# Four attention and expert layers in one kernel: a shorter start, and attention without loops in the first and the last layer

## The chip, the cores and the metric

The kernel runs on one core of a Trainium2 chip. The metric is the time of one execution on the device, in microseconds; three runs of the kernel before gave 761.37, 761.84 and 765.79, with a median of 761.84. Lower is better.

## The reference

Four layers follow each other on a residual stream x of 1024 tokens (4 sequences of 256) by 128 features. Each layer adds a cross-attention to a context of 4 x 64 tokens and then a mixture of experts:

```
x = x + xattn_0(layernorm(x), ctx, ctx, fside)     # 16 heads of 8, bias fside (256 x 64)
x = x + ffn_0(layernorm(x))                        # 8 experts, top 2, capacity 320
x = x + xattn_1(ctx, ctx, layernorm(x))            # exponential features
x = x + ffn_1(layernorm(x))                        # 16 experts that choose 64 tokens, shared expert
x = x + xattn_2(...);  x = x + ffn_2(layernorm(x)) # 16 heads of 8; 16 experts, top 2, dense
x = x + xattn_3(layernorm(x), ctx, ctx)            # 16 heads of 64
x = x + ffn_3(layernorm(x))                        # 8 experts, top 1
```

The attention of layers 0 and 3 is, per head h:

```
q = xn Wq_h,  k = ctx Wk_h,  v = ctx Wv_h
P = softmax(q k^T * scale + bias);  out = concat_h(P v) Wo
```

## The kernel before

Tokens lie in T = 8 tiles of 128 rows. Every engine has its own program, and the order of the work is written out by hand; the engines meet only in semaphores. Two tiles are in flight, with buffers j = 0 and 1 (scores in PSUM banks 2j and 2j + 1, turned probabilities in banks 4 and 5, outputs in bank 6 + j).

**Start.** GpSimd (POOL) makes some forty constants, among them `ident`, the head masks `hm8`, `hm16`, `hm64`, and clears `Vb`; its last instruction (L414) raises `const`, and all engines wait for that. SyncE queues the loads: x, the context three times, `aw0` (the attention weights of layer 0), `fside`, the rest, then padding stores and the expert weights of layer 0. VectorE (DVE) runs `setup()` (L1565 to L1598), and then `stats(0)`, the layer norm's mean and variance; GpSimd raises the variance to -0.5 (L457).

**Keys.** The query weights are folded into the keys: `A[:, b, h, :] = Wq_h^T k_h`, so that scores are one matmul of the turned, normalised x with A. For it TensorE (PE) projects the context (L594) into bank 0, ScalarE (ACT) copies it to `projT`, GpSimd multiplies each of 4 sequences' keys by the head mask into 16 blocks of 64 columns (`kblk`, L429), TensorE multiplies those by Wq (L603, eight matmuls of 128 rows and 512 columns), and ScalarE copies them into A. `v_sb` counts the copies of the values into `Vb`, where each head has 9 columns, the last a one that yields the softmax's sum.

**Attention of layers 0 and 3.** For a tile: `norm_x` (DVE, L1619), transpose (PE, L650), `x_out` (ACT), scores (PE, L653), `softmax_in` (DVE, L1629 to L1639: scale and bias in layer 0, maxima, subtract), `exp` (ACT, L1318), in layer 3 `den` (DVE, L1650 and L1652) and `normalise` (POOL, L545), `turn` (PE, eight transposes, L667), `turned` (ACT), `values` (PE, L682 with 18 columns or L679 with 128), in layer 0 `norm_out` (DVE), `turn_out` (PE, L689), `out_turned` (ACT), `project` (PE, L695), and `residual` (DVE, L1672). Each engine has a function `tile_step`, of which four run inside a hardware loop of two turns. TensorE's step for tile g is: transpose and scores of tile g + 2, turn g, turn out g - 1, values g, project g - 1. VectorE's is: norm_x g + 2, norm_out g - 1 (or den g), softmax_in g + 1, residual g - 1. The layers 1 and 2 have attention functions of their own.

After the attention comes `stats(1)`, `route(0)` (xn, router matmuls L887, maxima from L1817), and the experts.

## Time and profile before

| | |
|---|---|
| median of 3 runs | 761.84 us (761.37 to 765.79) |
| the profiled execution | 759.42 us, span 757.3 us |
| busy in the span | PE 491.4 (65%), DVE 303.0 (40%), ACT 176.8 (23%), POOL 182.1 (24%) |
| mean granted TensorE clock | 0.81 of 2.4 GHz |
| the chain that ended last | PE 44%, DVE 19%, issue 12%, POOL 9%, DMA 8%, ACT 7% |
| DMA | 42.15 MB, mean 56 GB/s |

Busy shares are means over stages with different limits. The chain of waits goes back from the last instruction to what released it, and its shares say who held the end up.
### The profile page before, as it was taken

The numbers are of one execution on the slowest core, as the hardware profiler recorded it, in microseconds if no ns is written. First come the engines' busy times: TensorE is split into PE (matmuls) and PEld (weight loads), VectorE is DVE, ScalarE is ACT, GpSimd is POOL, SyncE is SP. The second block draws the span as 40 slices with busy tenths as digits, with TensorE's granted clock in tenths as the row PEclk, the third lists the DMA queues.
The fourth block names the chain that finished last, engine by engine and source line by source line (L and its number), as shares of the span: only waits on it lengthen the run. The fifth ranks groups of instructions, "written<-read, shape, count | busy, mean of one in ns | idle before, by whom it ended". The sixth has DMA issues, their size and how long they took to land.

```text
span 757.3 us, 7336 instructions
## 1 busy us (share of the span) xinstructions
PE 491.4 (65%) x2438; PEld 301.5 (40%) x2440; DVE 303.0 (40%) x754; ACT 176.8 (23%) x366; POOL 182.1 (24%) x194
## 2 busy tenths in 40 slices
PE   1788842267925886664678816758997978650883
PEld 1265631244712444442345513433333535440562
DVE  1755546501243454477122212645442067531221
ACT  1432300022410311200132312302113533300431
POOL 6400000074570000000355531000002623314232
PEclk9997755577976897585899975959999999955897
DMA  7700000032440000101266520000103020003200
GB/s 233 270 1 0 1 29 2 1 83 89 164 128 1 0 1 1 32 0 29 60 198 198 151 60 1 1 0 1 33 30 148 1 90 0 0 1 110 65 13 4
DMA packets 29459, 42.15 MB, mean 56 GB/s; under 512 B 7060, under 2 KB 23581, under 8 KB 29298
## 3 DMA queue, kind: packets, MB, share of 16 engines
...
## 4 chain that ended last, share of the span: by engine, by line
PE 44%; DVE 19%; issue 12%; POOL 9%; DMA 8%; ACT 7%; another core or an unknown queue 0%; POOLq 0%; DVEq 0%; ACTq 0%; SPq 0%
DMA residual<-eo,idx 4%; PE bank L653 3%; PE bank L982 3%; PE bank L747 3%; DMA xgr<-rows,idx 2%; PE bank L990 2%; PE bank L1027 2%; DVE ind L1941 2%; PE bank L1031 2%; POOL pr L545 2%; PE bank L682 2%; PE bank L887 2%; PE bank L1023 2%; DVE PT L1723 2%; PE bank L903 2%
## 5 line engine op out<-in xcount | busy, mean ns | idle before, releaser
L457 POOL TENSOR_TENSOR rstd<-ve,neghalf 128x8 f32<-128x8 f32 x8 | 13.2, 1652 | 211.2 <-DVE ve L1562 211.1
L1239 ACT ACTIVATE PT<-bank 128x512 f32<-128x512 f32 x48 | 27.2, 596 | 74.9 <-PE bank L667 54.3
L653 PE MATMUL bank<-A,xaT 128*128 128x512 f32 (+1 forms) x64 | 37.6, 718 | 7.5 <-ACT xaT L1239 7.5
L448 POOL TENSOR_TENSOR kblk<-projT,hm 128x512 f32<-128x512 f32 x16 | 16.7, 1041 | 85.5 <-ACT projT L1239 85.4
L520 POOL DMA_INDIRECT residual<-eo,idx x16 | 25.3, 1579 | 36.6 <-DMA residual<-eo,idx 21.0
L2027 DVE SCALAR_TENSOR_TENSOR PT<-bank,xgr,sg 128x512 f32<-128x512 f32 x16 | 12.0, 751 | 51.8 <-ACT sg L1470 51.8
L491 POOL DMA_INDIRECT A<-rows,from_row x20 | 19.2, 960 | 53.1 <-DVE from_row L1875 47.3
L903 PE MATMUL bank<-ind,ones_bf 128*128 128x56 bf16 (+1 forms) x160 | 12.9, 240 | 29.3 <-DVE ind L1941 29.3
L982 PE MATMUL bank<-pr,wbig 128*128 128x320 f32 x64 | 26.1, 497 | 7.4 <-issue 6.7
...
L2056 DVE TENSOR_TENSOR PT<-bank,sg 128x352 f32<-128x352 f32 x15 | 7.9, 525 | 49.8 <-ACT sg L1504 49.8
L667 PE MATMUL bank<-ident,pr 128*128 128x128 f32 x128 | 19.8, 305 | 11.1 <-POOL pr L545 8.8
L667 PEld LDWEIGHTS bank<-ident,pr 128*128 128x128 f32 x128 | 16.8, 159 | 21.6 <-issue 9.7
L497 POOL DMA_INDIRECT choices<-eo,to_row x20 | 19.7, 987 | 21.4 <-DVE eo L1992 17.4
L545 POOL TENSOR_TENSOR pr<-pr,rden 128x1024 f32<-128x1024 f32 x8 | 15.2, 1902 | 39.9 <-DVE rden L1652 39.9
L903 PEld LDWEIGHTS bank<-ind,ones_bf 128*128 128x128 bf16 x160 | 9.6, 120 | 37.0 <-DVE ind L1941 36.4
L571 POOL DMA_INDIRECT result<-lg,Vb x15 | 14.8, 984 | 39.8 <-DVE lg L2061 39.8
L990 PE MATMUL bank<-PT,wbig 128*128 128x320 f32 x64 | 24.1, 467 | 0.0
L2001 DVE COPY yT<-bank 128x320 f32<-128x320 f32 x8 | 3.9, 491 | 48.0 <-PE bank L990 48.0
L1984 DVE TENSOR_TENSOR PT<-bank,sg 128x512 f32<-128x512 f32 x16 | 11.1, 692 | 29.0 <-ACT sg L1421 29.0
L1239 ACT ACTIVATE A<-bank 128x512 f32<-128x512 f32 (+1 forms) x24 | 12.6, 526 | 39.2 <-PE bank L823 22.7
L747 PE MATMUL bank<-A,kblk 128*128 128x512 f32 x32 | 19.4, 753 | 3.1 <-ACT kblk L1362 3.1
...
## 6 DMA issues: line engine op xcount, KB each, us to landing
...
wbig<-in_fw SPq DMA_DIRECT2D x8, 512.0 KB
wbig<-in_aw SPq DMA_DIRECT2D x1, 2048.0 KB, 10.0
...
```

The lines of the kernel that those rows point to most:

```text
L448: pool.tensor_tensor(out=kblk[:, c % 2, 0:512].rearrange("p (b h k) -> p b h k", b=B, h=2), in0=projT[:, c % 2, :].rearrange("p (b k) -> p ...
L491: pool.indirect_dma_start(xgr0[:, 5 * p + k, :], None, rowd0, bass.IndirectOffsetOnAxis(from_row[:, 5 * p + k:5 * p + k + 1], 0)).then_inc ...
L497: pool.indirect_dma_start(yd, bass.IndirectOffsetOnAxis(to_row[:, 5 * p + k:5 * p + k + 1], 0), eo0[:, 5 * (p % 2) + k, :], None, bounds_c ...
L520: pool.indirect_dma_start(xd, bass.IndirectOffsetOnAxis(idx[:, e:e + 1], 0), eo[:, e % 3, :], None, compute_op=ALU.add).then_inc(S("added" ...
L545: pool.tensor_tensor(out=pr[:, j], in0=pr[:, j], in1=rden[:, j, :].unsqueeze(2).broadcast_to([P, H, KEYS]), op=ALU.mult).then_inc(S("pnorm ...
L653: mm = pe.matmul(bank[2 * j + c][:, :], xaT[:, j, :], A[:, b, 8 * c:8 * c + 8, :].rearrange("p h k -> p (h k)"), start=True, stop=True)
L667: mm = pe.transpose(bank[4 + half][:, q * P:(q + 1) * P], pr[:, j, 2 * c:2 * c + 2, :].rearrange("p h k -> p (h k)"), ident[:, :])
L747: pe.matmul(bank[4 + c][:, :], qf1[:, b % 2, c, k * P:(k + 1) * P], A[:, b, 8 * c:8 * c + 8, :].rearrange("p h k -> p (h k)"), start=True, ...
L903: mm = pe.matmul(bank[4][:, 0:7 * e], ones_bf[:, :], ind[:, t, 0:7 * e], start=(t == 0), stop=(t == T - 1))
L982: pe.matmul(bank[s % 2][:, 0:CAP[0]], wring[:, e % 4, m * P:(m + 1) * P], xgT0[:, (e // 2) % 2, cols], start=True, stop=True).then_inc(S(" ...
L990: pe.matmul(bank[6 + e % 2][:, 0:CAP[0]], wring[:, e % 4, 512 + m * P:512 + (m + 1) * P], hh[:, s % 4, 0:CAP[0]], start=(m == 0), stop=(m ...
L1239: return act.activation(dst, src, ACT.Copy)
```

## The change

- **Start.** GpSimd makes `neghalf`, `ident` and `hm8` and then raises `const`; all other constants move into `later_constants()`, behind the power for the layer norm, and raise `const` a second time, which VectorE awaits in `setup()` and TensorE ahead of layer 0's router. `Vb` is cleared only in its first 576 columns. x is loaded in two halves; ctx_sb and aw0 go through ScalarE's queue; layer 0's expert weights are queued ahead of the padding stores. ScalarE copies one element (`table_try`) as soon as `const` is there.
- **Keys.** The projected keys are masked by VectorE straight out of bank 0 (`mask_keys0`) with the mask hm4, in which row p is one in column (p / 8) mod 4: 4 blocks instead of 16, for two sequences at a time. Four matmuls (`keys0`), each with its own 32 rows of Wq and of the masked keys, give 4 heads each in banks 4 to 7. ScalarE copies two of the first four, VectorE the other two; the second four are made and copied inside the attention.
- **Values.** One semaphore step for four matmuls, two copies instead of eight.
- **Set-up.** `setup()` moves behind the xn of layer 0's router, except for hm4.
- **Attention of layers 0 and 3.** No hardware loops. TensorE transposes tile t + 2, turns t, and only then makes the scores of t + 2. VectorE adds the residual of t - 2 and not of t - 1. In layer 3 turn and values are those of tile t - 1.

```diff
-            sp.dma_start(x[:, :, :], x_in.rearrange("(t p) d -> p t d", p=P)).then_inc(S("x_in"), 16)
-            sp.dma_start(ctx_sb[:, :], ctxT).then_inc(S("ctx_in"), 16)
+            x_t = x_in.rearrange("(t p) d -> p t d", p=P)
+            sp.dma_start(x[:, 0:4, :], x_t[:, 0:4, :]).then_inc(S("x_in"), 16)
+            sp.dma_start(x[:, 4:8, :], x_t[:, 4:8, :]).then_inc(S("x_back"), 16)
...
-            sp.dma_start(aw0_sb[:, :, :], aw0).then_inc(S("aw0_in"), 16)
-            sp.dma_start(fside_sb[:, :, :], fside.rearrange("(j p) k -> p j k", p=P)).then_inc(S("aw0_in"), 16)
+            sp.dma_start(fside_sb[:, :, :], fside.rearrange("(j p) k -> p j k", p=P)).then_inc(S("ctx_in"), 16)
...
+            for u in range(4):
+                load_weights(0, u, u)
             sp.wait_ge(S("rowpad"), 1)
...
-            for u in range(4):
-                load_weights(0, u, u)
...
+            chain(pool.memset(hm8[:, :], 1.0))
+            chain(pool.affine_select(out=hm8[:, :], in_=hm8[:, :], compare_op=ALU.is_ge, fill=0.0,
+                                     base=0, pattern=[[-8, 16]], channel_multiplier=1))
+            pool.affine_select(out=hm8[:, :], in_=hm8[:, :], compare_op=ALU.is_ge, fill=0.0,
+                               base=7, pattern=[[8, 16]], channel_multiplier=-1).then_inc(S("const"), 1)
+            pool.wait_ge(S("const"), 1)
+
+            def later_constants():
+
+                chain(pool.memset(rowpad[:, 0:256], 0.0))
+                pool.memset(rowpad[:, 256:ROW].bitcast(I32), 1 << 20).then_inc(S("rowpad"), 1)
...
+                pool.iota(pair_id, pattern=[[2, 8], [1, 2], [0, 64]], base=0, channel_multiplier=0,
+                          allow_small_or_imprecise_dtypes=True).then_inc(S("const"), 1)
...
-                if ND[layer] == 8:
...
+                chain(pool.memset(Vb[:, 0:B * H * (n + 1)], 0.0))
...
+                elif layer == 0:
+                    clear_values(0)
+                    rsqrt(0)
+                    later_constants()
...
-                        with pool.Fori(0, T // 2) as i:
-                            for j in range(2):
-                                normalise(2 * i + j, j, None)
+                        for t in range(T):
+                            normalise(t, t % 2, None)
...
+            def keys0(half):
+                pe.wait_ge(S("kblk"), half + 1)
+                for i in range(4):
+                    rows0 = slice(32 * i, 32 * i + 32)
+                    if half:
+                        pe.wait_ge(S("a_sb") if i < 2 else S("kblk"), i + 1)
+                    pe.matmul(bank[4 + i][:, :], aw0_sb[rows0, 0, :], kblk[rows0, 1, half * 512:(half + 1) * 512],
+                              start=True, stop=True).then_inc(S("kmm"), 1)
...
                     pe.wait_ge(S("aw0_in"), 32)
-                    pe.matmul(bank[0][:, 0:BK], w[:, 1, :], ctx_sb[:, :], start=True, stop=True).then_inc(S("proj"), 1)
+                    pe.matmul(bank[0][:, 0:BK], aw0_sb[:, 1, :], ctx_sb[:, :], start=True, stop=True).then_inc(S("proj"), 1)
+                    keys0(0)
+                    pe.wait_ge(S("ctx_in"), 48)
                     for b in range(B):
-                        pe.matmul(bank[1][:, b * D:(b + 1) * D], ctx_dup[:, b].rearrange("p s k -> p (s k)"), w[:, 2, :],
-                                  start=True, stop=True).then_inc(S("vproj"), 1)
-                    for b in range(B):
-                        pe.wait_ge(S("kblk"), EARLIER["kblk"][layer] + b + 1)
-                        for c in range(2):
-                            if b >= 2:
-                                pe.wait_ge(S("a_sb"), EARLIER["a_sb"][layer] + 2 * (b - 2) + c + 1)
-                            pe.matmul(bank[2 + 2 * (b % 2) + c][:, :], w[:, 0, :], kblk[:, b % 2, c * 512:(c + 1) * 512],
-                                      start=True, stop=True).then_inc(S("kmm"), 1)
+                        mm = pe.matmul(bank[3][:, b * D:(b + 1) * D], ctx_dup[:, b].rearrange("p s k -> p (s k)"), aw0_sb[:, 2, :],
+                                       start=True, stop=True)
+                    mm.then_inc(S("vproj"), 1)
...
+                def turn_x(g, j):
                     pe.wait_ge(S("at_lg"), g + 1)
                     pe.wait_ge(S("at_xn"), g + 3)
                     pe.transpose(bank[2 * j][:, 0:P], xa[:, j, :], ident[:, :]).then_inc(S("at_xT"), 1)
+
+                def scores(g, j, b):
                     pe.wait_ge(S("at_xTc"), g + 3)
...
-                def tile_step(g, j, b, ahead, first=False):
-
-                    if ahead is not None:
-                        front(g + 2, j, ahead)
-                    turn(g, j)
-                    if not first and layer != 3:
-                        turn_out(g - 1, 1 - j)
-                    values(g, j, b)
-                    if not first and layer != 3:
-                        project(g - 1, 1 - j)
...
+                back = 1 if layer == 3 else 0
+                for t in range(-2, T + 1):
+                    if layer == 0 and t == -1:
+                        keys0(1)
+                    if t + 2 < T:
+                        turn_x(G0 + t + 2, t % 2)
+                    if layer == 0 and t == -1:
+                        pe.wait_ge(S("v_sb"), 2)
+                    if layer == 0 and t == 0:
+                        pe.wait_ge(S("a_sb"), 6)
+                    if 0 <= t - back < T:
+                        turn(G0 + t - back, (t - back) % 2)
+                    if t + 2 < T:
+                        scores(G0 + t + 2, t % 2, (t + 2) // 2)
+                    if layer != 3 and t >= 1:
+                        turn_out(G0 + t - 1, (t - 1) % 2)
+                    if 0 <= t - back < T:
+                        values(G0 + t - back, (t - back) % 2, (t - back) // 2)
+                    if layer != 3 and t >= 1:
+                        project(G0 + t - 1, (t - 1) % 2)
...
+            def keys0(half, groups):
+                for i in groups:
+                    act.wait_ge(S("kmm"), 4 * half + i + 1)
+                    copy(A[:, 2 * half:2 * half + 2, 4 * i:4 * i + 4, :],
+                         bank[4 + i][:, :].rearrange("p (b j k) -> p b j k", b=2, j=4)).then_inc(S("a_sb"), 1)
...
+                back = 1 if layer == 3 else 0
+                for t in range(-2, T + 1):
+                    if t + 2 < T:
+                        x_out(G0 + t + 2, t % 2)
+                    if layer == 0 and t == -2:
+                        values0()
+                    if layer == 0 and t == -1:
+                        keys0(1, range(4))
+                    if 0 <= t - back < T:
+                        turned(G0 + t - back, (t - back) % 2)
+                    if layer != 3 and t >= 1:
+                        out_turned(G0 + t - 1, (t - 1) % 2)
+                    if 0 <= t + 1 < T:
+                        exp(G0 + t + 1, (t + 1) % 2)
...
+            act.dma_start(ctx_sb[:, :], ctxT).then_inc(S("aw0_in"), 16)
+            act.dma_start(aw0_sb[:, :, :], aw0).then_inc(S("aw0_in"), 16)
             act.wait_ge(S("const"), 1)
+            copy(table_try[:, :], neghalf[:, 0:1])
...
+                    if n == 0 and t == 4:
+                        dve.wait_ge(S("x_back"), 16)
...
+                if n == 0:
+                    mask_keys0()
                 dve.wait_ge(S("ln_rstd"), n + 1)
 
+            def mask_keys0():
+                dve.wait_ge(S("proj"), 1)
+                dve.wait_ge(S("hm4"), 1)
+                for half in range(2):
+                    dve.tensor_tensor(
+                        out=kb0[:, 2 * half:2 * half + 2, :, :],
+                        in0=bank[0][:, half * P:(half + 1) * P].rearrange("p (b k) -> p b k", b=2).unsqueeze(2).broadcast_to([P, 2, 4, KEYS]),
+                        in1=hm4[:, :].unsqueeze(1).unsqueeze(3).broadcast_to([P, 2, 4, KEYS]), op=ALU.mult).then_inc(S("kblk"), 1)
+
+            def keys0():
+                for i in range(2, 4):
+                    dve.wait_ge(S("kmm"), i + 1)
+                    dve.tensor_copy(A[:, 0:2, 4 * i:4 * i + 4, :], bank[4 + i][:, :].rearrange("p (b j k) -> p b j k", b=2, j=4)
+                                    ).then_inc(S("kblk"), 1)
...
-                def tile_step(t, j, first=False, ahead=True, last=False):
-                    g = t + G0
-                    if ahead:
-                        norm_x(g + 2, j, t + 2)
+                for t in range(-2, T + 2):
+                    if t + 2 < T:
+                        norm_x(G0 + t + 2, t % 2, t + 2)
+                    if layer == 0 and t == -2:
+                        keys0()
                     if layer == 3:
-                        den(g, j)
-                    elif not first:
-                        norm_out(g - 1, 1 - j, t - 1)
-                    if not last:
-                        softmax_in(g + 1, 1 - j)
-                    if not first:
-                        residual(g - 1, 1 - j, t - 1)
...
+                        if 0 <= t < T:
+                            den(G0 + t, t % 2)
+                    else:
+                        if 0 <= t - 1 < T:
+                            norm_out(G0 + t - 1, (t - 1) % 2, t - 1)
+                        if t >= 2:
+                            residual(G0 + t - 2, t % 2, t - 2)
+                    if 0 <= t + 1 < T:
+                        softmax_in(G0 + t + 1, (t + 1) % 2)
+                    if layer == 3 and t >= 2:
+                        residual(G0 + t - 2, t % 2, t - 2)
...
+                if layer == 0:
+                    setup()
...
-            setup()
+            dve.tensor_reduce(hm4[:, :], hm8[:, :].rearrange("p (i j) -> p j i", i=4), AX.X, ALU.add).then_inc(S("hm4"), 1)
```

What moves, in the order of instructions. TensorE at the start of the program (`aw_sb` is aw0), before:

```order
L594 MATMUL bank<-ctx_sb,aw_sb 128x256
L596 MATMUL bank<-aw_sb,ctx_dup 128x128 x4
L603 MATMUL bank<-kblk,aw_sb 128x512 x8
L650 MATMUL bank<-ident,xa 128x128
L653 MATMUL bank<-A,xaT 128x512 x2
```

and in the change:

```order
L599 MATMUL bank<-ctx_sb,aw_sb 128x256
L581 MATMUL bank<-kblk,aw_sb 128x512 x4
L603 MATMUL bank<-aw_sb,ctx_dup 128x128 x4
L650 MATMUL bank<-ident,xa 128x128
L655 MATMUL bank<-A,xaT 128x512 x2
L581 MATMUL bank<-kblk,aw_sb 128x512 x4
L650 MATMUL bank<-ident,xa 128x128
```

Half of the key matmuls (now L581, 32 rows each) stand behind the first tile's scores, and the values' matmuls behind the first four.

VectorE in layer 0's attention, one step, before:

```order
L1619 TENSOR_SCALAR xa<-x,mv,rstd 128x128
L1658 RECIPROCAL rden<-bank 128x16
L1662 TENSOR_TENSOR on<-bank,rden 128x128
L1629 SCALAR_TENSOR_TENSOR lg<-bank,fside_sb 128x512 x2
L1636 TENSOR_REDUCE mx<-lg 128x8 x2
L1639 TENSOR_TENSOR lg<-lg,mx 128x512 x2
L1672 TENSOR_TENSOR x<-bank,x 128x128
```

and in the change:

```order
L1635 TENSOR_SCALAR xa<-x,mv,rstd 128x128
L1676 RECIPROCAL rden<-bank 128x16
L1680 TENSOR_TENSOR on<-bank,rden 128x128
L1690 TENSOR_TENSOR x<-bank,x 128x128
L1647 SCALAR_TENSOR_TENSOR lg<-bank,fside_sb 128x512 x2
L1654 TENSOR_REDUCE mx<-lg 128x8 x2
L1657 TENSOR_TENSOR lg<-lg,mx 128x512 x2
```

The residual (x) stands ahead of the softmax and is that of one tile earlier.

TensorE in layer 3's attention, the first step that turns probabilities, before:

```order
L650 MATMUL bank<-ident,xa 128x128
L653 MATMUL bank<-A,xaT 128x512 x2
L650 MATMUL bank<-ident,xa 128x128
L653 MATMUL bank<-A,xaT 128x512 x2
L667 MATMUL bank<-ident,pr 128x128 x8
L679 MATMUL bank<-Vb,PT 128x128 x8
```

and in the change:

```order
L650 MATMUL bank<-ident,xa 128x128
L655 MATMUL bank<-A,xaT 128x512 x2
L650 MATMUL bank<-ident,xa 128x128
L669 MATMUL bank<-ident,pr 128x128 x8
L655 MATMUL bank<-A,xaT 128x512 x2
L681 MATMUL bank<-Vb,PT 128x128 x8
```

The first turn comes one tile later, and the scores stand between turn and values.

## Rows read from the trace of the kernel before

**Rows 1.** Timeline, the start: start us, us, engine, line, what [idle before <-releaser].
```profile
0.79 0.44 SPq L272 DMA_DIRECT2D x<-in_x_in  x1
...
11.59 3.51 POOL L414 MEMSET Vb<- 128x4096 f32 x1
...
15.16 1.22 PE L594 MATMUL bank<-ctx_sb,aw_sb 128*128 128x256 f32 x2 [15.16 <-POOL Vb L414]
...
18.29 3.88 POOL L429 TENSOR_TENSOR kblk<-projT,hm 128x1024 f32<-128x1024 f32 x2 [2.76 <-ACT projT L1239]
...
22.34 1.62 DVE L1555 BATCH_NORM_STATS2 st<-x 128x6 f32<-128x128 f32 x8
...
24.68 1.63 DVE L1562 TENSOR_SCALAR ve<-mv 128x8 f32<-128x8 f32 x1
...
26.45 1.68 POOL L457 TENSOR_TENSOR rstd<-ve,neghalf 128x8 f32<-128x8 f32 x1 [0.17 <-DVE ve L1562]
...
29.76 1.98 PE L653 MATMUL bank<-A,xaT 128*128 128x512 f32 x4 [0.43 <-ACT xaT L1239]
...
31.79 1.29 DVE L1629 SCALAR_TENSOR_TENSOR lg<-bank,fside_sb 128x512 f32<-128x512 f32 x2 [3.02 <-PE bank L653]
```

**Rows 2.** DMA issues up to 60 us; columns: what, count, KB each, us to landing.
```profile
x<-in_x_in SPq DMA_DIRECT2D x1, 512.0 KB, 4.2
aw_sb<-in_aw SPq DMA_DIRECT2D x2, 256.0 KB, 3.2
```

**Rows 3.** The timeline, a step and a slower step of layer 0's attention.
```profile
49.87 0.29 DVE L1672 TENSOR_TENSOR x<-bank,x 128x128 f32 x1 [3.20 <-PE bank L695]
...
51.36 1.98 PE L653 MATMUL bank<-A,xaT 128*128 x4 [0.47 <-ACT xaT L1239]
...
56.98 0.29 DVE L1672 TENSOR_TENSOR x<-bank,x 128x128 f32 x1 [2.14 <-PE bank L695]
...
66.13 0.29 DVE L1672 TENSOR_TENSOR x<-bank,x 128x128 f32 x1 [3.82 <-PE bank L695]
```

**Rows 4.** Stretches: from:to, us, busy by engine, TensorE clock, DMA share, GB/s.
```profile
15.00:18.00 3.00, 2.84 (x10) 2.45 (x10) 2.72 (x22) 1.52 (x2) 0.41 (x3) 1.00 1.03 382
...
66.00:73.00 7.00, 5.73 (x13) 3.27 (x14) 4.84 (x10) 0.86 (x2) 0.00 (x0) 0.52 0.00 0
...
605.85:666.98 61.13, 44.65 (x232) 30.23 (x232) 35.37 (x64) 19.93 (x34) 15.21 (x8) 0.94 0.08 28
```

**Rows 5.** The timeline, end of layer 0's attention and the router after it.
```profile
98.11 0.29 DVE L1672 TENSOR_TENSOR x<-bank,x 128x128 f32<-128x128 f32 x1 [1.78 <-PE bank L695]
...
109.96 0.23 DVE L1817 TENSOR_REDUCE rm<-bank 128x8 f32<-128x64 f32 x1 [4.83 <-PE bank L887]
```

**Rows 6.** The timeline, layer 3's attention: one tile, and the last.
```profile
611.73 1.06 ACT L1318 ACTIVATE pr<-lg 128x1024 f32<-128x1024 f32 x1 [0.90 <-DVE lg L1639]
...
625.56 1.22 DVE L1650 TENSOR_REDUCE rden<-pr 128x16 f32<-128x1024 f32 x1 [1.88 <-ACT pr L1318]
...
627.15 1.90 POOL L545 TENSOR_TENSOR pr<-pr,rden 128x1024 f32<-128x1024 f32 x1 [4.48 <-DVE rden L1652]
...
631.94 1.22 DVE L1650 TENSOR_REDUCE rden<-pr 128x16 f32<-128x1024 f32 x1 [1.89 <-ACT pr L1318]
...
656.32 1.06 ACT L1318 ACTIVATE pr<-lg 128x1024 f32<-128x1024 f32 x1
...
666.69 0.29 DVE L1672 TENSOR_TENSOR x<-bank,x 128x128 f32<-128x128 f32 x1 [7.63 <-PE bank L679]
```

**Rows 7.** The timeline, TensorE, the row-tiled scores of layer 1.
```profile
244.47 0.71 PE L763 MATMUL bank<-kblk,A 32*128 32x256 f32 x8
```

**Rows 8.** Matmuls before 45 us, grouped by line and form.
```profile
L594 PE MATMUL bank<-ctx_sb,aw_sb 128*128 128x256 f32 x2 | 1.2, 714 | 15.2 <-POOL Vb L414 15.2
```

**Rows 9.** Matmuls by line and form, 575 to 605 us.
```profile
L620 PE MATMUL bank<-ctx_sb,wbig 128*128 128x256 f32 x32 | 9.9, 398 | 1.2 <-issue 1.2
```

**Rows 10.** The page's costliest groups: busy us, mean ns | idle before, releaser.
```profile
L1239 ACT ACTIVATE PT<-bank 128x512 f32<-128x512 f32 x48 | 27.2, 596 | 74.9 <-PE bank L667 54.3
```

196 lines of the change are left out of this document (64 added, 132 removed).

## The prediction

> **What bounds the kernel now.** I read the windows first, then the timeline of the two stretches that the change touches, then the waits in them. Nothing outside layer 0's start, its attention, the router behind it and layer 3's attention is edited, so only these can pay directly.
>
> The start waits for GpSimd. TensorE's first matmul carries an idle time of 15.16 us, released by the last of GpSimd's constants (11.59 + 3.51) [rows 1], although x takes only 4.2 us from issue at 0.79 [rows 1, 2]. Then the keys go round projT, four products of GpSimd (two rows like the one at 18.29, each 3.88 for two) and eight matmuls. VectorE does its set-up from 15.1 to 22.3 and only then starts the statistics. The first score is worked on at 31.79 [rows 1].
>
> In layer 0's attention one tile takes from one residual add to the next: 49.87 to 56.98, 7.1 us, and 56.98 to 66.13, 9.15 us [rows 3]. VectorE has to issue the residual of tile t-1 before it normalises tile t+2, and that residual waits for TensorE's last matmul of the step, so TensorE stands still until the new tile has come through VectorE, its own transpose and ScalarE. The stretch 66 to 73 has a granted clock of 0.52, the level of 1.2 GHz, after TensorE's pause at the end of a step [rows 4]. The attention ends at 98.11 + 0.29 = 98.4 [rows 5].
>
> In layer 3 a step lasts 631.94 - 625.56 = 6.38 us and is a ring: exp 1.06, sum and reciprocal 1.59 until GpSimd starts, product 1.90, transposes, PSUM copies, and the next exp queued behind those copies on ScalarE [rows 6]. TensorE is busy 44.65 of 61.13 us, 5.6 per tile [rows 4].
>
> **Part 1, the start, until the first op on a score (31.79 now).** Of GpSimd's constants only six small ones stay ahead; the 3.51 us memset shrinks to 576 of 4096 columns, 0.5 us. So the loads bound. The first half of x lands at 0.79 + 4.2 = 5.0 at most, the second 0.44 later, 5.45 [rows 1, 2]. Eight statistics cost 1.62; the last four end at 6.3, the aggregates and ve (22.34 + 1.62 to 24.68 now, 0.7, and ve itself, whose 1.63 is a stall) bring 7.2 [rows 1]. aw0 now goes through ScalarE's queue, behind ctx: no row shows that queue. Its bounds are 3.2 (the same 256 KB on SyncE) and x's 4.2 after an issue at about 1.5, so 4.7 to 5.7 [rows 2], and the projection adds 1.22 [rows 1]: 6.9, hidden behind 7.2. The two masks are half as long as a pair of 128x512 ops, 0.65 each [rows 1]: the first is done at 7.85. rstd (1.68) runs beside them [rows 1].
>
> Keys: four row-tiled matmuls of 512 columns. Layer 1's four of 256 columns (eight records) together need 0.71 us [rows 7], while one full 128x512 needs 1.98 / 2 = 0.99 [rows 1], so four cost about 1.0, and 4.0 if they did not overlap. The clock: the granted clock of 15 to 18 us reads 1.00 [rows 4], yet the first matmul there has a mean of 714 ns where the same shape takes 398 later [rows 8, 9]. So the first ones run at the lower level, and I take 2.0: done at 9.85. The Trainium skill ("TensorE: Matmul & The Clock Gate", What's actually happening) says the default state is throttled and activity releases it. By that rule the start pays double; by the granted-clock record alone the forecast would be 1 us lower. The matmul rows agree with the rule.
>
> Copies out of PSUM, two deep on ScalarE (0.596 each [rows 10]) and two on VectorE, end at 11.1; TensorE meanwhile does four value matmuls, twice the columns of the projection's 1.22, 2.2 us: 12.0. Transpose and xaT 0.8, scores to first op 2.03 [rows 1]: **14.8**. Saved: 31.79 - 14.8 = **17.0**. Bounds: 12.5 (loads half a microsecond early, matmuls at full clock) and 18 (aw0 or x 3 us late).
>
> GpSimd's other constants, about 10 us of them, now run beside VectorE's first softmax. That VectorE can be held is in the trace: ve took 1.63 us and began in the GpSimd product that ended at 26.3 [rows 1]. Two or three small ops can be held for at most one constant each: I take **-0.5**, bounds 0 and -2. The Trainium skill ("SBUF — State Buffer", SBUF: two separate sides) makes it an exclusive lock for ops in a two-port mode or with two SBUF inputs, the latter only against a GpSimd op that reads SBUF. By it the subtracting ops are held by a few selects only, which stays inside the same bounds.
>
> **Part 2, layer 0's attention (66.6 us from 31.79 to 98.4).** TensorE now does transpose x, turn, scores, turn out, values, project, and VectorE adds the residual one tile later, ahead of the softmax. The copy of xaT hides behind turn, that of PT behind scores. A step of TensorE at full clock is what lies between 51.36 and 56.83 (just before the residual at 56.98), 5.5, plus the transpose, 0.3: 5.8 [rows 3]. VectorE needs 3 x 1.29 + 1.2 for the small ops = 5.0 and ScalarE less, so TensorE bounds. Count: softmax of tile 0 3.9, exp 1.06, a first step without out-transpose and projection 5.0: 10.0. Five full steps: 29. Then the last softmax waits for the fifth step's projection: 0.4 + 3.9 + 1.1 = 5.4, and turn, values, normalising, projection and residual 5.4: **49.8** with TensorE at full clock. A low stretch costs about the 2.05 us by which 9.15 exceeds 7.1 [rows 3]. TensorE no longer pauses between steps, so I expect one in the sparse ramp and a partial one in the tail: +3, **52.8**. Saved **13.8**. Bounds: 17 (none) and 5 (as many as now).
>
> **Part 3, layer 3 (61.1 us).** turn and values go one tile back, so the product has a whole step of time. The ring that is left is VectorE's: exp 1.06, sum and reciprocal 1.5, softmax input 2 x 1.29: 5.13 [rows 1, 6]. TensorE's 5.6 holds one slow last tile, about 5.3 without, and it has 4 us of slack before scores come late. Seven steps from the exp at 611.73 to the one at 656.32 save 7 x 1.25 = 8.7 [rows 6]. The tail, 656.32 to 666.98, ran with a slow last tile; it keeps its 10.7 or drops to 8.7: I take 1 less. Saved **9.6**, bounds 5 (TensorE at 5.6 to 5.8 and late) and 11.
>
> **Part 4, the rest.** setup() moves before VectorE's wait for the router, which idles 4.83 us there [rows 5]. It took 7.2 with GpSimd products beside it; two of its ops alone are about 1.9 each by the same stall, so 3.8 alone: hidden, cost 0. Without that cover it would cost 3.8. The padding stores start later and the expert weights earlier; both are needed after 150 us. The removed loops save a few branches, counted at 0. Everything behind layer 0 starts 30 us earlier, so the places where the clock falls can move: 0, bounds -3 and +3.
>
> **Sum.** 17.0 - 0.5 + 13.8 + 9.6 = 39.9. The profiled execution took 759.42 (span 757.3, 2.1 around it): 719.5. The median of the three runs is 2.4 above that execution, so I forecast **722**.
>
> **Rivals.**
> A. Layer 0's clock falls in every step as now. For it: low stretches recur there, and the values matmuls of 18 columns stay. Against: the pause ahead of each fall goes. Part 2 then saves 5 to 6: **730**. Chance 0.15.
> B. Layer 3 stays near its old step because TensorE, busy 5.6 per tile, with its hand-overs becomes the bound at 6.2. Against: the gaps there are waits for the product. It saves 2 instead of 9.6: **730**. Chance 0.12.
> C. Loads are late: two queues start at once and x, the doubled context and aw0 share the engines. The Trainium skill ("DMA: Bandwidth & Descriptors", Issuing engines are not separate DMA queues) says a second issuing engine saves only issue time. 3 to 5 us: **726**. Chance 0.08.
> D. Slower: TensorE stays at 1.2 GHz through both attentions because each now has few wide, dense matmuls in a row. A step is then twice 5.8 and twice 5.3: 8 x 11.6 + 10 = 103 against 66.6, and 8 x 10.6 + 5 = 90 against 61, so +65, minus 17 from the start: 762 + 48 = **810**. It decides once the steps, 8.3 and 6.4 on average now, pass 9.4 in layer 0 and 7.4 in layer 3, which eats the start's 17. For it: 66 to 73 stayed low although TensorE was busy 5.73 of 7 us [rows 4]. Against: layer 3 has a mean of 0.94. Chance 0.03.
> E. The time saved is given back behind it and nothing moves: 757. Only a wait on something absolute, such as a load, could do that, and none ends near. Chance 0.02.
>
> The forecast itself has 0.60. The range takes in the bounds of part 1 and one of A, B or C with a little of another: **713 to 737**. A measurement of this kernel tells about 1% from no change. Faster by more: 0.95, within 1%: 0.02, slower: 0.03.
>
> **What would show it.** The first op on a score at 13 to 16 us; GpSimd's constants ending near 20 with no TensorE wait on them; steps of 5.8 between residuals in layer 0 with a granted clock near 1; layer 0's attention ending near 68; steps of 5.1 to 5.3 between sums in layer 3; the idle before the router's maximum near 1 us. It would be wrong if TensorE's wait in layer 0 stays on the new tile, if the start waits on aw0 beyond 8 us, or if the clock is at 0.5 over most of either attention.

## The result, and the profile after

The changed kernel took 721.87 us, the median of four runs (716.18 to 727.98), and the kernel before beside it 763.5 (761.37 to 765.79): a ratio of 0.942, 95% interval 0.935 to 0.950. The forecast was 722. The ratio leaves out the run of 727.98, which is over 1.5% above the fastest of its kernel. These runs of the changed kernel fell into two groups some 9 us apart, and the granted clock went with them: 716.18 and 718.38 at 0.810 and 0.805 (a fifth, outside the median, took 718.41 at 0.805), 725.35 and 727.98 at 0.798 and 0.799. The profile below is of the 725.35 run (span 723.6), so it is set against 759.42 and span 757.3 of before: 33.7 us of span.

First the windows. They are cut where GpSimd begins rstd (the reciprocal standard deviation) of each layer norm, so that equal work stands in each. Before: layer 0's attention and norm, layer 2's attention, layer 2's experts, layer 3's attention, what follows. Columns: from:to, us, busy time (count) of PE, PEld, DVE, ACT, POOL, granted clock, DMA share, GB/s.

```profile
26.45:101.32 74.87, 56.56 (x260) 37.95 (x260) 41.08 (x97) 21.95 (x43) 1.68 (x2) 0.81 0.09 34
452.75:500.34 47.59, 28.82 (x224) 15.89 (x224) 22.42 (x49) 12.39 (x25) 3.71 (x4) 0.72 0.00 1
500.34:604.17 103.83, 91.41 (x271) 42.91 (x273) 36.39 (x85) 28.10 (x55) 18.29 (x17) 0.92 0.11 39
604.17:669.83 65.66, 45.79 (x240) 31.18 (x240) 37.84 (x81) 20.59 (x35) 16.85 (x9) 0.95 0.07 26
669.83:757.30 87.47, 46.32 (x250) 34.00 (x250) 17.94 (x59) 19.42 (x48) 25.49 (x27) 0.76 0.13 42
```

The same windows of the changed kernel:

```profile
8.51:70.26 61.75, 53.72 (x280) 39.27 (x280) 43.65 (x101) 24.86 (x48) 8.74 (x37) 0.85 0.39 132
420.60:474.56 53.96, 35.70 (x224) 18.76 (x224) 22.52 (x49) 12.40 (x25) 3.71 (x3) 0.59 0.00 0
474.56:579.91 105.35, 92.05 (x271) 43.21 (x273) 36.40 (x85) 28.04 (x55) 18.30 (x18) 0.91 0.11 38
579.91:634.57 54.66, 40.47 (x240) 29.42 (x240) 37.65 (x81) 20.52 (x35) 16.86 (x10) 1.00 0.09 31
634.57:723.60 89.03, 48.02 (x250) 35.07 (x250) 17.99 (x59) 19.44 (x48) 25.48 (x27) 0.74 0.13 41
```

The first rstd comes 26.45 - 8.51 = 17.9 us earlier, layer 0's stretch is 13.1 shorter, layer 3's 11.0. Layer 2's attention, whose code nobody touched, is **6.4 longer** with the same number of instructions: its TensorE is busy 35.7 us for 28.8, at a clock of 0.59 for 0.72. Behind it 1.5 and at the end 1.6 more are given back. The stages not shown (129.28, 76.10 and 146.05 before; 128.92, 76.30 and 145.12 now) save 1.1. Together 33.7: 17.9 + 13.1 + 11.0 - 6.4 - 1.5 - 1.6 + 1.1.

The start, TensorE and VectorE of the changed kernel (timeline: start, us, engine, line, what [idle before <-releaser]); it answers to [rows 1]:

```profile
6.16 1.19 PE L599 MATMUL bank<-ctx_sb,aw_sb 128*128 128x256 f32 x2 [6.16 <-DMA aw_sb<-in_aw]
9.02 2.09 PE L581 MATMUL bank<-kblk,aw_sb 32*128 32x512 f32 x8 [1.66 <-DVE kblk L1570]
11.04 2.08 PE L603 MATMUL bank<-aw_sb,ctx_dup 128*128 128x128 f32 x8
...
13.76 2.42 PE L655 MATMUL bank<-A,xaT 128*128 128x512 f32 x4 [0.43 <-ACT xaT L1239]
16.11 1.14 PE L581 MATMUL bank<-kblk,aw_sb 32*128 32x512 f32 x8
...
6.60 0.87 DVE L1554 BATCH_NORM_STATS2 st<-x 128x6 f32<-128x128 f32 x4 [1.78 <-DMA x<-in_x_in]
...
16.21 1.29 DVE L1647 SCALAR_TENSOR_TENSOR lg<-bank,fside_sb 128x512 f32<-128x512 f32 x2 [3.19 <-PE bank L655]
```

The wait for GpSimd is gone; loads release both engines. (The rows of a matmul group count its passes: an fp32 matmul is two of them.) The same eight row-tiled matmuls take 2.09 at 9.02 and 1.14 at 16.11. The first score is worked on at 16.21.

Layer 0's attention, on TensorE two turns of probabilities that waited, then one whole step and the first of the tail, and some of VectorE's residuals; it answers to [rows 3] and [rows 5]:

```profile
31.42 1.71 PE L669 MATMUL bank<-ident,pr 128*128 128x128 f32 x8 [0.44 <-ACT pr L1319]
...
43.52 1.09 PE L669 MATMUL bank<-ident,pr 128*128 128x128 f32 x8 [0.44 <-ACT pr L1319]
...
48.29 0.27 PE L650 MATMUL bank<-ident,xa 128*128 128x128 f32 x1
48.40 1.04 PE L669 MATMUL bank<-ident,pr 128*128 128x128 f32 x8
49.27 1.88 PE L655 MATMUL bank<-A,xaT 128*128 128x512 f32 x4
50.99 0.27 PE L691 MATMUL bank<-ident,on 128*128 128x128 f32 x1
51.10 1.86 PE L684 MATMUL bank<-Vb,PT 128*128 128x18 f32 x16
52.80 0.47 PE L697 MATMUL bank<-aw_sb,onT 128*128 128x128 f32 x2
53.94 1.09 PE L669 MATMUL bank<-ident,pr 128*128 128x128 f32 x8 [0.66 <-ACT pr L1319]
55.43 3.39 PE L684 MATMUL bank<-Vb,PT 128*128 128x18 f32 x16 [0.29 <-ACT PT L1239]
...
43.08 0.28 DVE L1690 TENSOR_TENSOR x<-bank,x 128x128 f32<-128x128 f32 x1
...
48.67 0.28 DVE L1690 TENSOR_TENSOR x<-bank,x 128x128 f32<-128x128 f32 x1
...
53.49 0.28 DVE L1690 TENSOR_TENSOR x<-bank,x 128x128 f32<-128x128 f32 x1
...
67.11 0.29 DVE L1690 TENSOR_TENSOR x<-bank,x 128x128 f32<-128x128 f32 x1 [1.47 <-PE bank L697]
```

No releaser stands on TensorE inside the last step, which lasts 53.49 - 48.67 = 4.82 us. The step ahead of it took 48.67 - 43.08 = 5.59: there TensorE waited 0.44 us for an exponential. The two lengths take turns, so a step is 5.2 us on average. Only the step from 30.94 to 38.26 took longer, 7.32, with the granted clock at 0.50 from 32 to 34 us. Two pauses open the tail, 0.66 and 0.29 us; from then on the values take 3.39 for 1.86. The router's maximum was read at 78.92, after an idle of 1.03 (4.83 before), 11.81 us behind the last residual (11.85 before).

Layer 3: an exponential on ScalarE, two sums on VectorE, and the last residual; it answers to [rows 6]:

```profile
597.65 1.06 ACT L1319 ACTIVATE pr<-lg 128x1024 f32<-128x1024 f32 x1 [2.79 <-DVE lg L1657]
...
593.65 1.22 DVE L1668 TENSOR_REDUCE rden<-pr 128x16 f32<-128x1024 f32 x1 [0.87 <-ACT pr L1319]
...
598.74 1.22 DVE L1668 TENSOR_REDUCE rden<-pr 128x16 f32<-128x1024 f32 x1 [0.87 <-ACT pr L1319]
...
631.36 0.29 DVE L1690 TENSOR_TENSOR x<-bank,x 128x128 f32<-128x128 f32 x1 [4.21 <-PE bank L681]
```

Exponential waits for the softmax input and the sum for the exponential: the ring of VectorE and ScalarE, 5.09 us a step. GpSimd's product releases nobody in these steps (TensorE waits for it, 0.99 us, only for the last two tiles).

### The profile page after: what moved, and what is told of

Read it like the earlier page. It is cut to its first block, busy times and chain, and to the rows that moved or that the text cites. A ratio compares the mean times of both kernels' runs of the same rounds, so it can differ in the third digit from the quotient of the medians.

```text
span 723.6 us, 7100 instructions
## 1 busy us (share of the span) xinstructions
PE 484.3 (67%) x2438; PEld 301.4 (42%) x2440; DVE 301.3 (42%) x758; ACT 174.8 (24%) x358; POOL 171.8 (24%) x190
## 4 chain that ended last, share of the span: by engine, by line
PE 39%; DVE 21%; issue 16%; DMA 10%; POOL 6%; ACT 5%; another core or an unknown queue 1%; POOLq 0%; SPq 0%; DVEq 0%; ACTq 0%
DMA residual<-eo,idx 6%; PE bank L981 3%; PE bank L746 3%; PE bank L989 2%; PE bank L1030 2%; PE bank L1026 2%; DVE ind L1952 2%; PE bank L849 2%; PE bank L886 2%; PE bank L1022 2%; DVE PT L1732 2%; POOL rstd L451 2%; PE bank L902 2%; DMA xgr<-rows,idx 2%; PE bank L836 2%
## 5 line engine op out<-in xcount | busy, mean ns | idle before, releaser
L655 PE MATMUL bank<-A,xaT 128*128 128x512 f32 x64 | 32.2, 627 | 2.4 <-ACT xaT L1239 2.4
L515 POOL DMA_INDIRECT residual<-eo,idx x16 | 25.3, 1582 | 35.7 <-DMA residual<-eo,idx 24.0
L1319 ACT ACTIVATE pr<-lg 128x1024 f32<-128x1024 f32 x16 | 16.9, 1057 | 28.4 <-DVE lg L1657 28.4
L1239 ACT ACTIVATE A<-bank 128x512 f32<-128x512 f32 (+1 forms) x22 | 11.0, 522 | 46.2 <-PE bank L822 26.1
L1415 ACT ACTIVATE sg<-bank 128x512 f32<-128x512 f32 x18 | 10.6, 597 | 46.4 <-PE bank L1026 46.4
L746 PE MATMUL bank<-A,kblk 128*128 128x512 f32 x32 | 19.4, 758 | 3.1 <-ACT kblk L1356 3.1
```

What stands on the lines that cost most here:

```text
L515: pool.indirect_dma_start(xd, bass.IndirectOffsetOnAxis(idx[:, e:e + 1], 0), eo[:, e % 3, :], None, compute_op=ALU.add).then_inc(S("added" ...
L655: mm = pe.matmul(bank[2 * j + c][:, :], xaT[:, j, :], A[:, b, 8 * c:8 * c + 8, :].rearrange("p h k -> p (h k)"), start=True, stop=True)
L746: pe.matmul(bank[4 + c][:, :], qf1[:, b % 2, c, k * P:(k + 1) * P], A[:, b, 8 * c:8 * c + 8, :].rearrange("p h k -> p (h k)"), start=True, ...
L1239: return act.activation(dst, src, ACT.Copy)
L1319: act.activation(pr[:, j], lg[:, j], ACT.Exp, scale=(1.0 if layer == 0 else SCALE[layer])).then_inc(S("at_p"), 1)
```

## The experiments

Two theories stand against each other. **Order**: each attention was a ring through TensorE, and moving one or two operations by a tile breaks it; the start gains by what it no longer waits for. **Surroundings**: hardware loops with their register waits, or a better clock, pay for it. Since whole times carry the two levels, I read each variant by stage. Each row is the one profiled execution of that kernel: the first op on a score; from there to the start of layer 0's last residual; from there to the router's maximum; the windows of layer 2's and layer 3's attention; the rest. The ratio is to the kernel before on the same chip, with its interval.

| kernel | first op | layer 0 | router | layer 2 | layer 3 | rest | ratio |
|---|---|---|---|---|---|---|---|
| before | 31.79 | 66.32 | 11.85 | 47.59 | 65.66 | 87.47 | 1 |
| changed | 16.21 | 50.90 | 11.81 | 53.96 | 54.66 | 89.03 | 0.942 (0.935-0.950) |
| after_again | 14.63 | 49.07 | 11.81 | 53.72 | 54.65 | 89.07 | 0.935 (0.926-0.943) |
| after_third | 16.53 | 48.78 | 11.81 | 47.67 | 54.66 | 89.25 | 0.942 (0.937-0.947) |
| l3_old | 17.11 | 48.59 | 11.81 | 47.65 | 65.66 | 87.67 | 0.951 (0.944-0.958) |
| l3_noloop | 15.78 | 50.07 | 11.81 | 53.97 | 63.97 | 89.18 | none |
| l3_back0 | 14.45 | 49.28 | 11.80 | 47.74 | 66.35 | 87.59 | 0.944 (0.935-0.952) |
| l0_old | 20.27 | 67.87 | 11.81 | 47.49 | 54.65 | 89.01 | 0.975 (0.966-0.984) |
| l0_noloop | 15.44 | 60.53 | 11.81 | 47.40 | 54.65 | 89.07 | 0.955 (0.947-0.964) |
| both_old | 20.34 | 64.96 | 11.81 | 47.43 | 65.64 | 87.50 | 0.978 (0.970-0.986) |
| setup_late | 14.84 | 48.33 | 15.61 | 47.47 | 54.66 | 89.19 | 0.940 (0.933-0.948) |
| fill_tail | 16.74 | 47.43 | 10.68 | 47.04 | 54.65 | 89.12 | 0.941 (0.933-0.949) |
| early_loads_fill2 | 14.94 | 48.79 | 11.81 | 53.01 | 54.66 | 89.21 | 0.939 (0.931-0.947) |
| warm | 15.29 | 49.12 | 10.70 | 47.39 | 54.67 | 89.10 | 0.939 (0.933-0.946) |

The kernel before had medians of 752.83 us beside l3_old, l0_old, both_old and setup_late, 771.04 beside after_again, l3_noloop, l3_back0 and l0_noloop, 765.02 beside fill_tail and early_loads_fill2, and 765.62 beside warm and after_third. So times of different groups are not compared. The four runs of l3_noloop (721.59 to 736.75) fall so far apart that no ratio is given; it is read by stage alone.

**l3_old.** Layer 3's attention on the four engines as before, loops included:

```diff
+                if layer in (3,):
...
+                    front(G0, 0, 0)
+                    front(G0 + 1, 1, 0)
+                    tile_step(G0, 0, 0, 1, first=True)
+                    with pe.Fori(0, T // 2 - 2) as i:
+                        tile_step(2 * i + (G0 + 1), 1, i, i + 1)
+                        tile_step(2 * i + (G0 + 2), 0, i + 1, i + 2)
...
+                else:
                     back = 1 if layer == 3 else 0
                     for t in range(-2, T + 1):
```

> Layer 3's attention in its old order on all four engines (scores ahead of the turned softmax, values of the same tile, residual one tile later, hardware loops); all else as changed. If layer 3's gain is the order's, as Part 3 of the prediction has it, the step between two sums goes back from 5.09 to about 6.3 us, the stretch from the first row normalised to the last residual from 50.1 to about 60 us, and the time rises by 9 to 11 us (to some 732). If the gain was the clock's (0.94 granted before, 1.00 after), the old order at a clock of 1.00 gives a step near 5.6 and some 4 us.

The window went from 54.66 back to 65.66, to the hundredth what it was before, and the rest came back 1.4 shorter: 9.6 in all, and the step is back at 6.38. That is the order theory's number. The whole time says less (its interval overlaps the changed kernel's).

**l0_old.** The same for layer 0, the second half of the keys and all values made ahead of it.

```diff
+                if layer in (0,):
+                    if layer == 0:
+                        keys0(1)
+                        pe.wait_ge(S("v_sb"), 2)
+                        pe.wait_ge(S("a_sb"), 6)
...
+                    front(G0, 0, 0)
+                    front(G0 + 1, 1, 0)
+                    tile_step(G0, 0, 0, 1, first=True)
```

> Layer 0's attention in its old order with its loops, all keys and values of the new start made ahead of it; the start and layer 3 as changed. By Part 2 the stretch from the first score operation to the last residual goes back from 51.2 to between 62 and 67 us and the time rises by 10 to 15 us (to some 734). The rival: the old attention was slow because of what stood around it (key and value preparation that trickled in), then the old order gives some 55 us and the time rises by under 5 us. The first score operation should come 1 to 3 us later than 16.2 us, since the second half of the keys is no longer behind it.

67.87 us, just over the upper edge; the first op came 4 us later, not 1 to 3. The ratio's interval, 0.966 to 0.984, lies above the changed kernel's. The rival's 55 is out.

**both_old.** Both edits. What is left is the start and the moved set-up.

```diff
+                if layer in (0, 3):
```

> Both attentions in their old order: of the change only the new start and the moved set-up are left. If the parts add, the time is 10 + 13 us above the changed kernel's, 743 to 750 us, which is 13 to 18 us under the kernel before. If the start's 15.6 us were given back later (by the clock or by loads that came too late), it is above 752 us.

17.0 us under the kernel before beside it (735.83 against 752.83), inside the expected 13 to 18; the absolute 743 to 750 was missed, since this whole group ran some 10 us lower. The first op came at 20.34: with all keys made ahead the start saves 11.4 us, and putting half of them into the attention gives another 3 to 6.

**setup_late.**

```diff
-                if layer == 0:
-                    setup()
                 dve.wait_ge(S("router"), layer + 1)
+                if layer == 0:
+                    setup()
```

> VectorE's set-up of layer 0's routing placed behind its wait for the router instead of ahead of it; all else as changed. If the wait covered it, as the prediction has it (3.8 us uncovered), the router's maximum comes some 3.7 us later after the last normalised row and the time rises by 3 to 4 us. If something else held the router's maximum, nothing moves.

VectorE, between the last normalised row and the router's maximum:

```profile
74.97 0.15 DVE L1584 TENSOR_SCALAR sgn_i<-chan_i 128x1 int32<-128x1 int32 x1 [4.83 <-PE bank L886]
...
78.78 0.21 DVE L1828 TENSOR_REDUCE rm<-bank 128x8 f32<-128x64 f32 x1
```

The idle of 4.83 is back ahead of the set-up, and the set-up's 3.8 us now come after it: the maximum is 15.61 - 11.81 = 3.8 late. The stage shows it; the whole time does not (0.940 with an interval of 0.933 to 0.948 cannot tell 4 us).

**after_again.** The changed kernel unedited, as level.

```diff
+# the changed kernel once more
```

> The changed kernel once more, as the level that its variants of the same call are set against. Stages by the profile as in its first execution (61.8 to the router of layer 0, 54.7 for layer 3's attention), but layer 2's attention near 47.5 us, as every other kernel had it, instead of 54.0, if its lower clock there was that one execution's.

Its layer 2 window was 53.72 again, so the 53.96 was **not** one execution's accident. Over all runs there are two values, 47.0 to 47.7 and 53.0 to 54.0. Of the eleven executions with the changed attention order or its straight variants in layer 0, four show the upper one; the three with layer 0's old order show the lower, which with such counts may be chance.

**l3_noloop.** Straight, but scores ahead of the turn and values of the same tile.

```diff
-                back = 1 if layer == 3 else 0
+                back = 0
+                    if layer == 3 and t + 2 < T:
+                        scores(G0 + t + 2, t % 2, (t + 2) // 2)
                     if 0 <= t - back < T:
                         turn(G0 + t - back, (t - back) % 2)
```

> Layer 3's attention written straight, but in the old order (scores ahead of the turned softmax, values of the same tile). If the order gives the gain, the step between two sums is near 6.38 us and the stretch about 61 us, as with loops. If the hardware loops and their register waits cost it, the step is near 5.1 and the time that of the changed kernel. By the prediction the order gives nearly all: 6.2 to 6.4.

Two sums on VectorE:

```profile
601.14 1.22 DVE L1670 TENSOR_REDUCE rden<-pr 128x16 f32<-128x1024 f32 x1 [2.00 <-ACT pr L1321]
...
607.57 1.22 DVE L1670 TENSOR_REDUCE rden<-pr 128x16 f32<-128x1024 f32 x1 [2.00 <-ACT pr L1321]
```

607.57 - 601.14 = 6.43 us a step: the order. The loops cost nothing in the steps (6.38 with them). The window is still 1.7 shorter than with loops (63.97 against 65.66), and the values of the last tile, in the kernel before and in l3_noloop, show where:

```profile
662.90 3.76 PE L679 MATMUL bank<-Vb,PT 128*128 128x128 f32 x16
...
638.36 2.02 PE L681 MATMUL bank<-Vb,PT 128*128 128x128 f32 x16 [0.40 <-ACT PT L1241]
```

They ran at the lower clock before (0.50 from 661.83 to 665.83 us) and at the upper one here.

**l3_back0.** Straight, turn ahead of scores as in the change, only the lag of one tile taken out.

```diff
-                back = 1 if layer == 3 else 0
+                back = 0
-                    if layer == 3 and t >= 2:
-                        residual(G0 + t - 2, t % 2, t - 2)
+                    if layer == 3 and 1 <= t <= T:
+                        residual(G0 + t - 1, (t - 1) % 2, t - 1)
```

> Layer 3's attention straight, with the turned softmax ahead of the scores as in the change, but the values of tile t in step t instead of t+1. TensorE then waits in each step for exponential, sum, GpSimd's division and the turn's copies before it may begin the scores. If the lag of one tile is what counts, the step is 6.4 us or more (up to 7.5, since the scores now also stand behind the wait); if the split of the transposed input from the scores is enough, it is near 5.1.

TensorE:

```profile
595.52 1.09 PE L669 MATMUL bank<-ident,pr 128*128 128x128 f32 x8 [1.71 <-POOL pr L544]
...
601.94 0.33 PE L669 MATMUL bank<-ident,pr 128*128 128x128 f32 x1 [1.71 <-POOL pr L544]
```

GpSimd's product releases the turn each time, 6.42 us a step. The window is 66.35, so without the lag of one tile nothing of layer 3's gain is left. The lag with the old order of scores and turn was not run.

**l0_noloop.** Layer 0 straight, keys inside it as changed, but scores ahead of the turn and the residual behind the softmax.

```diff
+                    if layer == 0 and t + 2 < T:
+                        scores(G0 + t + 2, t % 2, (t + 2) // 2)
                     if 0 <= t - back < T:
                         turn(G0 + t - back, (t - back) % 2)
...
+                    if layer == 0 and t >= 1:
+                        residual(G0 + t - 1, (t - 1) % 2, t - 1)
```

> Layer 0's attention straight, its second half of keys made inside it as in the change, but the scores ahead of the turned softmax and the residual behind the next tile's softmax, as before. With loops and the old order the stretch from the first score operation to the last residual was 65 to 68 us, in the change 48 to 51. If the order gives the gain, it is 62 to 66 here and the time 12 to 15 us over the changed kernel's; if loops and register waits cost it, about 50.

TensorE, and VectorE's residuals around it:

```profile
41.41 0.30 PE L650 MATMUL bank<-ident,xa 128*128 128x128 f32 x1 [0.73 <-DVE xa L1637]
42.14 1.98 PE L655 MATMUL bank<-A,xaT 128*128 128x512 f32 x4 [0.43 <-ACT xaT L1241]
...
45.40 1.93 PE L684 MATMUL bank<-Vb,PT 128*128 128x18 f32 x16 [0.29 <-ACT PT L1241]
...
40.72 0.29 DVE L1692 TENSOR_TENSOR x<-bank,x 128x128 f32<-128x128 f32 x1 [2.09 <-PE bank L697]
...
47.68 0.29 DVE L1692 TENSOR_TENSOR x<-bank,x 128x128 f32<-128x128 f32 x1 [2.09 <-PE bank L697]
```

The ring of the prediction to the letter: residual, normalised x, transpose, copy, scores, ..., projection, residual, 6.96 us at a granted clock of 1.00, against 4.82 and 5.6 by turns. So the order gives 10 to 12 of the stretch's 14 to 20 us; scores and residual were moved back together, and what each gives alone was not run. What is left, 65 to 68 against 60.5, lies in loops, register waits, the low stretches and where the second half of the keys is made, and these were not told apart.

**fill_tail.** Extra matmuls of 128x512, read by nobody, where no scores are left and ahead of the router's transposes.

```diff
+            def keep_warm(banks):
+                for k in banks:
+                    pe.matmul(bank[k][:, :], ident[:, :], ctx_dup[:, :, :, :].rearrange("p b s k -> p (b s k)"), start=True, stop=True)
...
+                    if layer == 0 and t in (T - 2, T - 1):
+                        pe.wait_ge(S("at_lg"), t + 3)
+                        keep_warm([2 * (t % 2), 2 * (t % 2) + 1])
...
+                    if layer == 0:
+                        keep_warm([2, 3] * 2)
                     normed(layer)
```

> As changed, with eight extra matmuls of 128x512 whose output nobody reads: two each in the steps t = 6 and 7 of layer 0's attention, where no scores are left, and four between the attention and the transposes of the normalised rows (a gap of some 5 us). In the changed kernel the granted clock fell to 0.50 at 55.8 us behind two pauses of TensorE (0.66 and 0.29 us) and stayed there until layer 0's experts; values took 3.4 us for 1.9. If the pauses bring it down, the clock stays at 1.00 until the router, layer 0's attention ends 1 to 3 us earlier in spite of 3.8 us of added matmuls, the transposes and the router's products take 3 us less, and the time falls by 2 to 5 us. If the clock falls all the same, the extra matmuls cost 2 to 4 us.

TensorE, the first turn of the tail, values of two tiles, the last four extra matmuls and the router's transposes:

```profile
52.77 1.09 PE L673 MATMUL bank<-ident,pr 128*128 128x128 f32 x8 [0.66 <-ACT pr L1328]
...
55.53 1.86 PE L688 MATMUL bank<-Vb,PT 128*128 128x18 f32 x16
...
60.36 1.86 PE L688 MATMUL bank<-Vb,PT 128*128 128x18 f32 x16
...
64.68 5.18 PE L640 MATMUL bank<-ctx_dup,ident 128*128 128x512 f32 x8 [0.54 <-DVEq L2110]
69.69 1.83 PE L887 MATMUL bank<-ident,xn 128*128 128x128 f32 x8
```

The values stay at 1.86 where the changed kernel had 3.39 and 3.55, the attention is the shortest of all (47.43) though it holds 3.8 us of added matmuls, and the router's maximum comes 1.1 sooner. The clock stayed at 1.00 until 64 us and not, as expected, to the router: it fell behind the attention (the last four extra matmuls took 5.18 us, which is some 1.4 more than the four in the attention), and was back at 1.00 from 68. So the extra matmuls keep the clock up, but that the pauses bring it down is **not** shown: the 0.66 us pause stands here too, ahead of the first extra matmul, and no fall followed, and l0_noloop paused for 0.73, 0.43 and 0.29 us in each step at a granted clock of 1.00. The 0.29 us pause and the missing scores of the tail were not told apart. 1 to 3 us in the attention as expected; in whole time not to be told (0.941).

**early_loads_fill2.** Two edits far apart.

```diff
+            sp.wait_ge(S("x_back"), 16)
             for c in range(2):
...
+                keep_warm([3] * 15)
                 pe.wait_ge(S("kblk"), 12 + 2)
                 query(0)
```

> Two edits in stages far apart, read by stage. First: SyncE holds all loads behind x's second half until that has landed. If the start is bound by the loads sharing their bandwidth (x's second half was waited for until 6.60 us, the attention weights until 6.16), the first score operation comes 0.5 to 1.5 us earlier than 14.6 to 16.2 us; if each load's own latency binds it, nothing moves or the held loads come late for the values. Second: 15 extra matmuls of 128x512, some 14 us, fill TensorE's wait of 16 to 17 us ahead of layer 2's attention. If the idle stretch ahead is what decides between the two levels of that stage (47.5 us at a clock of 0.72, 53.8 us at 0.60), it takes at most 47.5 us with a clock over 0.72; if the matmuls run at the low clock they take 27 us and make that stage some 10 us later.

x's second half was used at 5.76 us (5.66, 5.84 and 6.60 in the three executions of the changed kernel) and the first op came at 14.94: no gain to be seen. TensorE and the granted clock around the second edit:

```profile
404.00:416.00 12.00, 12.00 (x30) 1.00 0.34 80
...
424.00:432.00 8.00, 5.05 (x24) 0.50 0.00 0
```

Of the gap of 16 us 13 were filled at a clock of 1.00, which left 2.9 idle, and still the clock fell inside the stage, which took 53.01 for the expected 47.5 at most. So filling the idle stretch ahead of the stage does not keep it at its lower value. Whether its own pauses decide is not shown; filling those was not tried.

**warm.** fill_tail, and twenty small matmuls in the start.

```diff
             pe.wait_ge(S("const"), 1)
+            for k in range(14):
+                pe.matmul(bank[7][:, 0:P], ident[:, :], ident[:, :], start=True, stop=True)
...
+                    for k in range(6):
+                        pe.matmul(bank[7][:, 0:P], ident[:, :], ident[:, :], start=True, stop=True)
                     keys0(0)
```

> The extra matmuls of the tail (as in fill_tail) and twenty of 128x128 at the start, 14 ahead of the key projection and 6 behind it, while TensorE waits for its weights and for the masked keys; no output of them is read. In three executions of the changed start the first scores' four passes took 1.98, 2.42 and 3.78 us for 1.88 later on, and keys and values 2.09 and 2.08 for 1.14 and 1.04. If that is TensorE's clock not yet being up, the keys and values ahead of the first score operation take 1.1 and 1.0 us, the scores 1.9, and that operation comes at 12.5 to 14 us instead of 14.5 to 17.1. If it is something else (the loads' traffic, new code), the durations stay and it comes 0 to 1 us later. With the tail's 2 to 3 us the whole is 3 to 6 us under the changed kernel, which is as much as separates its own two levels.

TensorE in the start:

```profile
2.46 5.74 PE L1221 MATMUL bank<-ident 128*128 128x128 f32 x28 [2.46 <-POOL hm L375]
8.04 0.60 PE L599 MATMUL bank<-ctx_sb,aw_sb 128*128 128x256 f32 x2
...
9.90 1.14 PE L581 MATMUL bank<-kblk,aw_sb 32*128 32x512 f32 x8
10.97 1.16 PE L605 MATMUL bank<-aw_sb,ctx_dup 128*128 128x128 f32 x8
```

Projection 0.60 for 1.19, keys 1.14 for 2.09, values 1.16 for 2.08, the first scores 1.98: the start does run at the lower level. But the first op did not come at 12.5 to 14 us as expected: fourteen were too many. They took 5.74 us and held the projection, whose weights came near 6 in the other executions, until 8.04. What the clock gave, the wait took, and the first op came at 15.29.

**after_third.** The level for warm: 720.67 us against 719.18, six runs each, with overlapping intervals.

```diff
+# the changed kernel, a third time
```

> The changed kernel again, as the level for the one above on this chip: 716 to 728 us, first score operation at 14.5 to 17.1 us, layer 2's attention stage at 47.5 or at 53.8 us.

No variant is shown to beat the changed kernel.

## Why the prediction held, and where it did not

| term | forecast | first execution | in the other runs |
|---|---|---|---|
| Part 1, start | 17.0 | 15.6 | 14.7 to 17.3 |
| GpSimd beside VectorE | -0.5 | within the above | |
| Part 2, layer 0 | 13.8 | 15.4 | 16.2 to 18.0 |
| Part 3, layer 3 | 9.6 | 11.0 | 11.0 |
| Part 4, set-up | 0 | 0.0 | 0 (3.8 uncovered) |
| Part 4, clock elsewhere | 0 | -9.5 | -1.5 to -1.9, or -8.5 to -9.6 |
| the three stages left | 0 | +1.1 | |
| sum | 39.9 | 33.7 | |

For the other runs of the start and of layer 0 the kernels whose code is the changed one up to there are taken; the clock's row is layer 2's attention, its experts and the rest. Forecast and first execution are of the profiled runs: 759.42 - 39.9 = 719.5 was forecast and 725.35 came, 5.9 more.

**The start.** The mechanism held: loads bound it, GpSimd's constants end at 19.4 and nobody waits. Two sizes were off and partly cancel. The weights arrived at 6.16, not 4.7 to 5.7, and x's second half was used at 6.60, not 5.45. The masks and the rest followed from there. Keys at 2.09 and values at 2.08 were as forecast, since the lower level had been priced in; the first scores were not: 2.42, and 1.98, 3.78 and 3.67 in other executions, for 1.88 later on. With the weights and the second half of x, which came at other times too (the keys began at 9.02, 8.25 and 8.08 in the three executions of the changed kernel), they let the first op wander between 14.5 and 17.1. warm turned the argument into a measurement. The Trainium skill ("TensorE: Matmul & The Clock Gate", What's actually happening) has it that the throttled state is the default one, and the durations agree, while the granted clock of the first 16 us reads 1.00 in every profile (0.99 in both_old).

**Part 2.** Right ring, wrong step. I took 5.8 us of TensorE per step, read from a stretch of the old order; it held a wait for a copy ahead of the values (0.23 in that step) and the drained end of the last group, and its scores and values took some 0.1 each more than now. The new order hides the copy and runs the groups into each other: the six durations at 48.29 to 52.80 sum to 5.79, but each group starts some 0.16 before the end of the one ahead, and start to start it is 4.82. (The Trainium skill, "TensorE: Matmul & The Clock Gate", Step-by-step: what each phase is for, says that the drain of one matmul overlaps the fill of the next. The 0.16 fits, but it is no proof, since the profile models the ends of matmuls.) Every second step TensorE waits for an exponential and takes 5.6, so the steps were some 0.6 too long in my sum, 5.8 for 5.2. Against that stood one step of 7.32 with a low stretch, which I had allowed for, and a tail that ran wholly at the lower clock (11.3 us from 55.8 to 67.1, of which fill_tail won back 1 to 3.5). Rival A, a fall in every step, did not come, nor rival D.

**Part 3.** l3_back0 and l3_noloop show that the gain needs the lag and not the straight code. The step is 5.09 (5.13 forecast), and seven of them saved 44.59 - 35.64 = 9.0 for 8.7. The tail from the last exponential to the end went from 10.7 to 8.5, 2.1 less where I had taken 1, and that is the clock: the last tile's turn and values took 1.97 and 3.76 us before and 1.09 and 2.02 now. The stretch behind gives 1.4 to 1.8 of it back in every kernel whose last tile ran at the upper clock (89.0 to 89.3 us) and not in the four where it ran at the lower one (before, l3_old, both_old and l3_back0, 87.5 to 87.7); why it does was not looked into. Rival B failed. In each full step TensorE now waits 0.3 to 0.6 us for VectorE's next normalised x, so VectorE's ring bounds and not TensorE.

**The clock elsewhere** is the term that was mis-sized. I had 0, with bounds of 3, and it was -9.5 in the first execution. Layer 2's attention takes one of two values some 6.3 us apart, and with it the experts behind it (0.8 to 1.6 apart); the third part is the 1.6 of the last window, the other side of layer 3's tail. The three profiled executions of the changed kernel are 725.35 and 721.87 with the upper value and 716.81 with the lower. The runs that were only timed have no trace, and in after_third they fill the range from 718.29 to 723.22 without a gap, so the two groups of the first four runs are not a rule.

That the median met the forecast of 722 so closely is luck. The sum of savings was some 6 too large: 1.6 and 1.4 too little in the attentions, 0.9 too much in the start, 9.5 lost to the clock and 1.1 gained in the three stages left. I had put the median 2.4 above the profiled run, as before the change, and it fell 3.5 below; that made up for the rest. For the same reason whole times here tell no edit of 4 us. Stages do: layer 3's window repeats to 0.02 us and the router's to 0.01, while layer 0's attention moves by 2.6.
